# Second scores of each half between M2 and M7, in a fused cross-attention kernel on one core

## Chip, core and metric

One NeuronCore of one Trainium2 chip. The metric is the device time of one launch in microseconds. The kernel before took 1660.45 us, the median of three runs (1659.76 to 1660.83).

## What is computed

One perceiver layer on a state x of 256 rows by 512: a cross-attention of x over a context of 25088 rows (8 heads of 64), a self-attention of 16 heads, and a mixture of 8 experts. Only the cross-attention is touched. Cut to that:

```
q = heads(layernorm(x) @ Wq.T + bq)        # 256 rows, 8 heads of 64
k = heads(ctx @ Wk.T + bk)                 # 25088 rows
v = heads(ctx @ Wv.T + bv)
x = x + softmax(q @ k.T / sqrt(64)) @ v    # over all 25088 rows
x = x + self_attention(layernorm(x))       # not touched
x = x + experts(x)                         # not touched
```

## The kernel before

**Chunks.** The context is cut into 49 chunks of 512 rows. Step c (from -1 to 49, the middle ones in a hardware loop of two steps each) does the attention of chunk c and makes K and V of chunk c + 1. Every product of two fp32 matrices is taken as three fp16 products of a high and a low part; so each tile is split after it is made: ScalarE writes the high part (`block_highs`, `p_highs`, `ctx_highs`), VectorE the low part as the difference (`block_lows`, `p_lows`), and GpSimd the low parts of the context (`ctx_sums`, `ctx_lows`, lines 363 to 380).

**Strassen.** K (h = 0) and V (h = 1) of a chunk, four 256x256 blocks each, are made with Strassen's seven products, `units` M1, M5, M6, M2, M7, M3, M4 of 12 matmuls each, in four PSUM banks `ps_proj` (line 1147). Between them other engines work on the banks: ScalarE's `seed` (L527, L529; waits for M1) and `copy_m5` (L538; waits for M5), VectorE's `add_u4` (L877, L880; waits for M6 and copy_m5) and `add_c22` (L887; waits for M7). M7 waits for add_u4. M4 waits for c22_done, since it writes the bank that add_c22 reads. A block is done after M2 (C11), M7 and add_c22 (C22), M3 (C12), M4 (C21); then `block_highs` and `block_lows` (L549 to L554 and L861 to L867) take it out. The next half's M1, M5 and seed wait for the low parts of C11, C22 and C12.

**Attention of a chunk** goes in four groups g of two heads, two in each half (g = 2h and 2h + 1). TensorE's `scores` (L1193) fill the two banks `ps_s`, which are there once, so they wait for the exponentials of the group before. VectorE's `maxima` are a reduction (L839) and the running maximum nmax (L846). ScalarE's `exps` (L573) are four exponentials with sums, `p_highs` is L584, VectorE's `p_lows` L852. SP turns both parts of P with a transposing DMA (`turn_p`, L293) and TensorE's `weigh` (PV, L1211) uses them two groups later. VectorE's `add_o` adds the result.

**Order.** There is no planner; each engine runs its own list in the order of the code, and semaphores join them. Per half h, before (groups 2h and 2h + 1):

- TensorE: M1, scores(2h), M5, M6, PV, M2, M7, scores(2h+1), M3, PV, M4.
- VectorE: C21 low of the half before, maxima(2h), p_lows(2h-1), add_u4, add_o, p_lows(2h), add_c22, C11 low, maxima(2h+1), C22 low, C12 low.
- ScalarE: C21 high of the half before, seed, p_highs(2h-1), alpha, copy_m5, exps(2h), p_highs(2h), C11 high, ctx_highs of chunk c + 2, C22 high, C12 high, exps(2h+1).
- GpSimd in the K half: four context sums (L363, L364, L366, L368), three low parts (L380), the rescaling of the accumulator (L420 to L425), the difference of maxima (L435). In the V half: four low parts (L380), of which all but the first wait for ScalarE's ctx_highs, the rescaling and the difference.

Of the kernel before, what the change touches and what calls it, by code (L numbers as in the profile page):

```python
# [56 lines left out]
def exists(c, n, count=NCH):  # L57

    return not isinstance(c, int) or 0 <= c + n < count


def after(c, n, least=0):

    return not isinstance(c, int) or c + n >= least


def back(c, u, lag, per=NG):

    return (c, u - lag) if u >= lag else (c - 1, u - lag + per)


def layer(nc, x, ctxt, wq, wk, wv, bv, cols, w_in, wg, w1, w2, w3, out):
    with ExitStack() as ctx:
# [141 lines left out]
        M1, M5, M6, M2, M7, M3, M4 = (0, 0, 0), (3, 3, 3), (4, 4, 1), (1, 1, 0), (5, 5, 1), (6, 2, 2), (2, 6, 1)  # L215
# [5 lines left out]
        def units_through(g):  # L221

            return UNITS * g - 6
# [16 lines left out]
        C11, C22, C12, C21 = (0, 0, 0), (3, 1, 1), (2, 0, 1), (1, 1, 0)  # L240

        def half_bank(n):

            return ps_proj[:, n, :].rearrange("p (t k) -> p t k", t=2)
# [213 lines left out]
        def _(act):  # L458
# [7 lines left out]
            def ctx_highs(k, odd, half):  # L466

                if half == 0:
                    act.wait_ge(ctx_loaded[odd], 8 * k + (16 - 8 * odd))
                    act.activation(ctx_s[odd][0][:, 0:2, :, :].rearrange("p b t k -> p (b t) k"), ctx_f[odd][:, :, 0:QUARTER],  # L470
                                   ACT.Copy).then_inc(ctx_high, 1)
                else:
                    act.activation(ctx_s[odd][0][:, 2, :, :], ctx_f[odd][:, 2:4, QUARTER:CH], ACT.Copy).then_inc(ctx_high, 1)
                act.wait_ge(t_sum, 4 * k - 1 + half)
                act.activation(ctx_s[odd][0][:, 3 + 2 * half:5 + 2 * half, :, :], t_f[:, 2 * half:2 * half + 2, :, :],  # L475
                               ACT.Copy).then_inc(t_high, 1)
# [88 lines left out]
            def exps(c, g, odd):  # L565

                act.wait_ge(nmax_done, NG * c + g + 1)
                if g % 2 == 0 and after(c, -2):
                    act.wait_ge(scaled, 2 * (c - 2) + g // 2 + 1)
                for b in range(2):  # L570
                    for r in range(2):
                        col = 4 * g + 2 * b + r
                        ins = act.activation(prob[:, g % 2, (2 * b + r) * HC:(2 * b + r + 1) * HC],  # L573
                                             ps_s[:, b, r * HC:(r + 1) * HC], ACT.Exp, bias=nmax[odd][:, col:col + 1],
                                             scale=LOGIT_SCALE, accum_out=lsum[odd][:, col:col + 1])
                ins.then_inc(exp_done, 1)
# [9 lines left out]
            def step(c, odd):  # L586
                for h in range(2):
                    strassen = exists(c, 1) and after(c, 0)
                    if exists(c, h) and after(c, h - 1):
                        block_highs(c + h, 1 - h, C21, odd if h == 0 else 1 - odd)  # L590
                    if not after(c, 0):
                        for g in range(NG):
                            plain_highs(h, g)
                        weight_sum_highs(h)
                    if strassen:
                        seed(c + 1, h)
                    pc, pg = back(c, 2 * h, 1)
                    if exists(pc, 0):
                        p_highs(pc, pg)
                    if exists(c, -1) and h == 0:  # L600
                        alphas(c - 1, 1)
                    if exists(c, 0) and h == 1:
                        alphas(c, 0)
                    if strassen:
                        copy_m5(c + 1, h)
                    if exists(c, 0):
                        exps(c, 2 * h, odd)
                    if exists(c, 0):
                        p_highs(c, 2 * h)
                    if strassen:  # L610
                        block_highs(c + 1, h, C11, 1 - odd)
                    if exists(c, 2):
                        ctx_highs(c + 2, odd, h)
                    if strassen:
                        for which in (C22, C12):
                            block_highs(c + 1, h, which, 1 - odd)
                    if exists(c, 0):
                        exps(c, 2 * h + 1, odd)
                    if isinstance(c, int) and c == LOOP_END + 1:
                        act.wait_ge(tisa_arg, h + 1)  # L620
                        act.activation(tisa_e[:, h, :], tisa_e[:, h, :], ACT.Exp).then_inc(tisa_exp, 1)
# [81 lines left out]
        def _(dve):  # L703
# [145 lines left out]
            def p_lows(c, g):  # L849

                dve.wait_ge(p_high, NG * c + g + 1)
                dve.scalar_tensor_tensor(out=p_s[:, g % 2, 1, :], in0=prob[:, g % 2, :], scalar=P_SCALE, in1=p_s[:, g % 2, 0, :],  # L852
                                         op0=ALU.mult, op1=ALU.subtract).then_inc(p_low, 1)
# [29 lines left out]
            def add_c22(k, h):  # L883

                g = 2 * k + h
                dve.wait_ge(unit_done, units_through(g) + 5)
                dve.tensor_tensor(half_bank(bank(h, 3)), half_bank(bank(h, 1)), m5_f[:, :, :], ALU.add).then_inc(c22_done, 1)  # L887
# [20 lines left out]
            def step(c, odd):  # L908
                for h in range(2):
                    strassen = exists(c, 1) and after(c, 0)  # L910
                    if exists(c, h) and after(c, h - 1):
                        block_lows(c + h, 1 - h, C21, odd if h == 0 else 1 - odd)
                    if not after(c, 0):
                        for g in range(NG):
                            plain_lows(h, g)
                        if h == 0:
                            split_q()
                            bias_rows()
                        weight_sum_lows(h)
                    if exists(c, 0):  # L920
                        maxima(c, 2 * h, odd)
                    pc, pg = back(c, 2 * h, 1)
                    if exists(pc, 0):
                        p_lows(pc, pg)
                    if strassen:
                        add_u4(c + 1, h)
                    if exists(c, -1):
                        add_o(c - 1, h)
                    if exists(c, 0):
                        p_lows(c, 2 * h)  # L930
                    if strassen:
                        add_c22(c + 1, h)
                        block_lows(c + 1, h, C11, 1 - odd)
                    if exists(c, 0):
                        maxima(c, 2 * h + 1, odd)
                    if strassen:
                        for which in (C22, C12):
                            block_lows(c + 1, h, which, 1 - odd)
                    if isinstance(c, int) and c == LOOP_END + 1:
                        tisa_args(h)  # L940
                    if isinstance(c, int) and c == NCH and h == 0:
                        tisa_scores()
# [146 lines left out]
        def _(pe):  # L1089
# [126 lines left out]
            def step(c, odd):  # L1216
                for h in range(2):
                    if not after(c, 0):
                        for g in range(NG):
                            if h == 0 and g == 2:  # L1220
                                turn(0)
                            plain(h, g)
                        if h == 0:
                            project_q()
                    if isinstance(c, int) and c == NCH and h == 0:
                        tisa_scores()

                    def units(*which):
                        for m in which:
                            if exists(c, 1) and after(c, 0):  # L1230
                                unit(c + 1, 1 - odd, h, m)

                    for half, before, between, behind in ((0, (M1,), (M5, M6), (M2, M7)), (1, (), (M3,), (M4,))):
                        g = 2 * h + half
                        units(*before)
                        if exists(c, 0):
                            scores(c, g, odd)
                        units(*between)
                        vc, vg = back(c, g, PV_LAG)
                        if exists(vc, 0):  # L1240
                            weigh(vc, vg, odd if g >= PV_LAG else 1 - odd)
                        units(*behind)
# [139 lines left out]
```

## Time and profile before

| | |
|---|---|
| median of three runs | 1660.45 us |
| profiled execution | 1662.99 us, span 1661.3 us |
| TensorE matmuls busy | 1566.8 us (94%) |
| TensorE weight loads busy | 1276.5 us (77%) |
| VectorE busy | 1323.7 us (80%) |
| ScalarE busy | 1268.4 us (76%) |
| GpSimd busy | 822.6 us (50%) |
| mean granted TensorE clock | 0.971 of full speed |

The busy times are over the whole span; the steps of the Strassen loop lie between about 43 and 1277 us of it. Within that stretch each chunk repeats the one before almost to the hundredth of a microsecond, so a single chunk can be read on the timeline (here the stretch from 800 to 827 us, a V half and a K half).

### The profile page before, as it was taken

The numbers are of one execution on the slowest core, as the hardware profiler recorded it, in microseconds if no ns is written. First come the engines' busy times: TensorE is split into PE (matmuls) and PEld (weight loads), VectorE is DVE, ScalarE is ACT, GpSimd is POOL, SyncE is SP. The second block draws the span as 40 slices with busy tenths as digits, with TensorE's granted clock in tenths as the row PEclk, the third lists the DMA queues.
The fourth block names the chain that finished last, engine by engine and source line by source line (L and its number), as shares of the span: only waits on it lengthen the run. The fifth ranks groups of instructions, "written<-read, shape, count | busy, mean of one in ns | idle before, by whom it ended". The sixth has DMA issues, their size and how long they took to land.

```text
span 1661.3 us, 47795 instructions
## 1 busy us (share of the span) xinstructions
PE 1566.8 (94%) x17748; PEld 1276.5 (77%) x17748; DVE 1323.7 (80%) x1764; ACT 1268.4 (76%) x3074; POOL 822.6 (50%) x938
## 2 busy tenths in 40 slices
PE   7899999999999999999999999999998687999998
PEld 5788888888888888888888888888876455777776
DVE  7788888888888888888888888888887466766765
ACT  4888888888888888888888888888886254655554
POOL 5667657666676576666765766667653000000000
PEclk9999999999999999999999999999999765999999
DMA  4365454454544544545445445454456630555551
GB/s 171 80 136 129 107 139 112 122 133 108 137 126 107 139 110 123 134 111 134 126 107 139 111 123 133 108 137 126 109 106 157 167 151 1 191 204 210 192 198 43
DMA packets 442690, 216.03 MB, mean 130 GB/s; under 512 B 416768, under 2 KB 422912, under 8 KB 436112
## 3 DMA queue, kind: packets, MB, share of 16 engines
q1 hardware_dynamic: 442352, 215.07, 48.1%
q8 instruction: 34, 0.56, 0.2%
q10 hardware_dynamic: 288, 0.27, 0.1%
q14 instruction: 16, 0.13, 0.0%
HBM read 111.96 MB, written 0.56 MB: 68 GB/s over the span
## 4 chain that ended last, share of the span: by engine, by line
DVE 33%; PE 25%; ACT 20%; issue 18%; DMA 1%; SPq 1%; DVEq 1%; ACTq 0%; POOL 0%; POOLq 0%
ACT prob L573 14%; DVE cmax L839 12%; PE ps_proj L1316 9%; DVE p_s L852 6%; DVE nmax L846 5%; PE ps_o L1339 5%; PE ps_proj L1147 4%; ACT p_s L584 3%; DVE k_s L864 2%; DVE ps_proj L877 2%; DVE v_s L861 2%; PE ps_s L1193 2%; ACT v_s L549 1%; PE ps_proj L1176 1%; PE ps_s L1272 1%
## 5 line engine op out<-in xcount | busy, mean ns | idle before, releaser
L1147 PE MATMUL ps_proj<-ctx_s,wk_s 128*128 128x256 f16 x4032 | 487.9, 273 | 30.5 <-DVE ps_proj L877 27.6
L1147 PE MATMUL ps_proj<-wv_s,ctx_s 128*128 128x256 f16 x4032 | 483.5, 274 | 1.2 <-ACT ps_proj L529 1.2
L1147 PEld LDWEIGHTS ps_proj<-ctx_s,wk_s 128*128 128x128 f16 x4032 | 376.5, 98 | 103.7 <-issue 63.1
L1147 PEld LDWEIGHTS ps_proj<-wv_s,ctx_s 128*128 128x128 f16 x4032 | 381.3, 98 | 64.6 <-issue 20.0
L573 ACT ACTIVATE prob<-ps_s,nmax 128x256 f32<-128x256 f32 x784 | 360.4, 473 | 77.0 <-DVE nmax L846 72.5
L380 POOL TENSOR_TENSOR ctx_s<-t_f,ctx_s 128x512 f16<-128x512 f32 x192 | 220.0, 1157 | 358.9 <-ACT ctx_s L475 358.9
L852 DVE SCALAR_TENSOR_TENSOR p_s<-prob,p_s 128x1024 f16<-128x1024 f32 x196 | 291.1, 1485 | 57.6 <-ACT p_s L584 57.6
L839 DVE TENSOR_REDUCE cmax<-ps_s 128x4 f32<-128x1024 f32 x196 | 238.1, 1215 | 3.8 <-PE ps_s L1193 3.8
L584 ACT ACTIVATE p_s<-prob 128x1024 f16<-128x1024 f32 x196 | 209.1, 1067 | 6.7
L380 POOL TENSOR_TENSOR ctx_s<-ctx_f,ctx_s 128x512 f16<-128x512 f32 x144 | 167.1, 1160 | 69.2 <-ACT ctx_s L470 69.2
L1316 PE MATMUL ps_proj<-x_s,wsp 128*128 128x256 f16 x1536 | 180.5, 275 | 4.2 <-issue 3.2
L1316 PEld LDWEIGHTS ps_proj<-x_s,wsp 128*128 128x128 f16 x1536 | 151.2, 99 | 36.6 <-issue 3.5
L861 DVE TENSOR_TENSOR v_s<-ps_proj,v_s 128x512 f16<-128x512 f32 x192 | 127.1, 681 | 64.7 <-ACT v_s L549 64.7
L1211 PE MATMUL ps_o<-v_s,pt_s 128*128 128x64 f16 x4704 | 171.2, 194 | 6.6 <-DMA pt_s<-p_s 6.6
L1193 PE MATMUL ps_s<-k_s,q_s 64*128 64x256 f16 x2352 | 163.8, 272 | 13.9 <-ACT prob L573 8.9
L1211 PEld LDWEIGHTS ps_o<-v_s,pt_s 128*128 128x128 f16 x4704 | 165.0, 99 | 14.4 <-DMA pt_s<-p_s 7.8
L573 ACT ACTIVATION_READ_ACCUMULATOR prob<-ps_s,nmax 128x1 f32 x784 | 161.1, 205 | 0.0
L965 DVE SCALAR_TENSOR_TENSOR wsp<-wst,wsp 128x1024 f16<-128x1024 f32 x96 | 114.6, 1222 | 47.9 <-ACT wsp L645 47.9
L1193 PEld LDWEIGHTS ps_s<-k_s,q_s 64*128 64x128 f16 x2352 | 99.2, 94 | 68.1 <-ACT prob L573 35.6
L549 ACT ACTIVATE v_s<-ps_proj 128x512 f16<-128x512 f32 x192 | 114.1, 595 | 39.2 <-PE ps_proj L1147 37.8
L867 DVE TENSOR_TENSOR k_s<-ps_proj,k_s 128x512 f16<-128x512 f32 x144 | 94.4, 681 | 61.6 <-ACT k_s L554 61.6
L846 DVE SCALAR_TENSOR_TENSOR nmax<-cmax,nmax 128x4 f32<-128x4 f32 x196 | 116.0, 592 | 8.6
(163 smaller groups left out, 1875.5 us busy)
## 6 DMA issues: line engine op xcount, KB each, us to landing
ctx_f<-ctxt_dram SPq DMA_DIRECT2D x48, 1024.0 KB, 5.1
wst<-w_dram SPq DMA_DIRECT2D x96, 512.0 KB, 4.7
pt_s<-p_s SPq DMA_TRANSPOSE x392, 2.7
w_in_sb<-w_in_dram SPq DMA_DIRECT2D x1, 3072.0 KB, 11.1
tisa<-tisa_scores SPq DMA_DIRECT2D x3, 1024.0 KB, 12.0
w_f<-wk_dram SPq DMA_DIRECT2D x2, 512.0 KB, 5.7
ctx_f<-ctxt_dram SPq DMA_DIRECT2D x2, 512.0 KB, 7.0
w_f<-wv_dram SPq DMA_DIRECT2D x1, 1024.0 KB, 9.9
```

The lines of the kernel that those rows point to most:

```text
L380: pool.tensor_tensor(out=low[:, n, :, :], in0=sources[n], in1=high[:, n, :, :], op=ALU.subtract).then_inc(ctx_low, 1)
L549: ins = act.activation(out_v(0, odd, i, j), ps, ACT.Copy)
L573: ins = act.activation(prob[:, g % 2, (2 * b + r) * HC:(2 * b + r + 1) * HC], ps_s[:, b, r * HC:(r + 1) * HC], ACT.Exp, bias=nmax[odd][:, ...
L584: act.activation(p_s[:, g % 2, 0, :], prob[:, g % 2, :], ACT.Copy, scale=P_SCALE).then_inc(p_high, 1)
L839: dve.tensor_reduce(cmax[:, g % 2, :], ps_s[:, :, :].rearrange("p b (r k) -> p (b r) k", r=2), AX, ALU.max).then_inc(cmax_done, 1)
L846: dve.scalar_tensor_tensor(out=nmax[odd][:, 4 * g:4 * g + 4], in0=cmax[:, g % 2, :], scalar=-LOGIT_SCALE, in1=nmax[1 - odd][:, 4 * g:4 * g ...
L852: dve.scalar_tensor_tensor(out=p_s[:, g % 2, 1, :], in0=prob[:, g % 2, :], scalar=P_SCALE, in1=p_s[:, g % 2, 0, :], op0=ALU.mult, op1=ALU. ...
L861: ins = dve.tensor_tensor(out_v(1, odd, i, j), ps, out_v(0, odd, i, j), ALU.subtract)
L1147: ins = pe.matmul(ps_proj[:, bank(h, role), sub * QUARTER:(sub + 1) * QUARTER], lhsT, rhs, start=(fresh and sub == 0 and t == 0 and i == 0 ...
L1193: ins = pe.matmul(ps_s[:, head, r * HC:(r + 1) * HC], q_s[a][rows, g, r * P:(r + 1) * P], k_s[odd][b][rows, g, r * HC:(r + 1) * HC], start ...
L1211: ins = pe.matmul(ps_o[:, vg // 2, col:col + DK], pt_s[:, vg, a, 4 * head + tile, :], v_s[vodd][b][:, tile, u * DK:(u + 1) * DK], start=(i ...
L1316: ins = pe.matmul(ps_proj[:, u % 2, m * T:(m + 1) * T], wsp[a][:, (u // 2) % 2, m, col:col + P], x_s[b][:, t, :], start=(t == 0 and k == 0 ...
```

## The change

In each half TensorE takes scores(2h+1) between M2 and M7; before they stood between M7 and M3. VectorE takes maxima(2h+1) ahead of p_lows(2h), and C11 low ahead of add_c22. ScalarE takes exps(2h+1) ahead of C22 high and C12 high. Which semaphore each operation waits for, and its count, stay as they are. The orders after are:

- TensorE: M1, scores(2h), M5, M6, PV, M2, scores(2h+1), M7, M3, PV, M4.
- VectorE: C21 low, maxima(2h), p_lows(2h-1), add_u4, add_o, maxima(2h+1), p_lows(2h), C11 low, add_c22, C22 low, C12 low.
- ScalarE: C21 high, seed, p_highs(2h-1), alpha, copy_m5, exps(2h), p_highs(2h), C11 high, ctx_highs, exps(2h+1), C22 high, C12 high.

```diff
@@ scalar, step @@
                     if exists(c, 2):
                         ctx_highs(c + 2, odd, h)
+                    if exists(c, 0):
+                        exps(c, 2 * h + 1, odd)
                     if strassen:
                         for which in (C22, C12):
                             block_highs(c + 1, h, which, 1 - odd)
-                    if exists(c, 0):
-                        exps(c, 2 * h + 1, odd)
@@ vector, step @@
                     if exists(c, 0):
+                        maxima(c, 2 * h + 1, odd)
+                    if exists(c, 0):
                         p_lows(c, 2 * h)
                     if strassen:
+                        block_lows(c + 1, h, C11, 1 - odd)
                         add_c22(c + 1, h)
-                        block_lows(c + 1, h, C11, 1 - odd)
-                    if exists(c, 0):
-                        maxima(c, 2 * h + 1, odd)
-                    if strassen:
                         for which in (C22, C12):
                             block_lows(c + 1, h, which, 1 - odd)
@@ tensor, step @@
-                    for half, before, between, behind in ((0, (M1,), (M5, M6), (M2, M7)), (1, (), (M3,), (M4,))):
+                    for half, before, between, behind in ((0, (M1,), (M5, M6), (M2,)), (1, (), (M7, M3), (M4,))):
```

## Rows read from the trace of the kernel before

**Rows 1.** The page's first line.

```profile
span 1661.3 us, 47795 instructions
```

**Rows 2.** Timeline 800 to 830 us, weight loads: start us, us, engine, line, count, [idle].

```profile
800.28 1.22 PEld L1147 LDWEIGHTS ps_proj<-ctx_s,wk_s 128*128 128x128 f16 x12
...
812.75 1.22 PEld L1147 LDWEIGHTS ps_proj<-wv_s,ctx_s 128*128 128x128 f16 x12
...
815.49 0.55 PEld L1193 LDWEIGHTS ps_s<-k_s,q_s 64*128 64x128 f16 x12 [0.21 <-ACT prob L573]
...
819.56 1.22 PEld L1147 LDWEIGHTS ps_proj<-ctx_s,wk_s 128*128 128x128 f16 x12
...
821.64 1.22 PEld L1147 LDWEIGHTS ps_proj<-ctx_s,wk_s 128*128 128x128 f16 x12 [0.86 <-issue]
...
823.07 0.55 PEld L1193 LDWEIGHTS ps_s<-k_s,q_s 64*128 64x128 f16 x12 [0.21 <-issue]
...
825.82 1.22 PEld L1147 LDWEIGHTS ps_proj<-ctx_s,wk_s 128*128 128x128 f16 x12
```

**Rows 3.** The same timeline, VectorE.

```profile
805.51 0.16 DVE L846 SCALAR_TENSOR_TENSOR nmax<-cmax,nmax 128x4 f32<-128x4 f32 x1
...
810.84 0.68 DVE L861 TENSOR_TENSOR v_s<-ps_proj,v_s 128x512 f16<-128x512 f32 x1
...
817.81 0.62 DVE L846 SCALAR_TENSOR_TENSOR nmax<-cmax,nmax 128x4 f32<-128x4 f32 x1
818.35 2.37 DVE L852 SCALAR_TENSOR_TENSOR p_s<-prob,p_s 128x1024 f16<-128x1024 f32 x1
820.65 0.87 DVE L877 SCALAR_TENSOR_TENSOR ps_proj<-ps_proj,bk_d,m_f 128x256 f32<-128x256 f32 x2
...
822.03 1.21 DVE L852 SCALAR_TENSOR_TENSOR p_s<-prob,p_s 128x1024 f16<-128x1024 f32 x1
823.17 0.70 DVE L887 TENSOR_TENSOR ps_proj<-ps_proj,m_f 128x512 f32<-128x512 f32 x1
823.78 0.87 DVE L864 SCALAR_TENSOR_TENSOR k_s<-ps_proj,bk_s,k_s 128x256 f16<-128x256 f32 x2
```

**Rows 4.** Timeline 1264.5 to 1268 us: scores and the reduction that waited for them.

```profile
1265.11 0.55 PEld L1193 LDWEIGHTS ps_s<-k_s,q_s 64*128 64x128 f16 x12 [0.21 <-issue]
...
1265.98 1.23 DVE L839 TENSOR_REDUCE cmax<-ps_s 128x4 f32<-128x1024 f32 x1 [0.24 <-PE ps_s L1193]
...
1267.24 0.91 DVE L846 SCALAR_TENSOR_TENSOR nmax<-cmax,nmax 128x4 f32<-128x4 f32 x1
```

**Rows 5.** Timeline 800 to 830 us, GpSimd.

```profile
811.09 1.16 POOL L380 TENSOR_TENSOR ctx_s<-t_f,ctx_s 128x512 f16<-128x512 f32 x1 [7.34 <-ACT ctx_s L475]
...
817.15 1.26 POOL L364 TENSOR_TENSOR t_f<-ctx_f 128x512 f32<-128x512 f32 x1
818.38 1.27 POOL L366 TENSOR_TENSOR t_f<-ctx_f,t_f 128x512 f32<-128x512 f32 x1
819.72 2.13 POOL L368 TENSOR_TENSOR t_f<-ctx_f,t_f 128x512 f32<-128x512 f32 x1
823.33 1.16 POOL L380 TENSOR_TENSOR ctx_s<-ctx_f,ctx_s 128x512 f16<-128x512 f32 x1 [1.48 <-ACT ctx_s L470]
```

**Rows 6.** The same timeline, ScalarE: first and last instruction of exps(0).

```profile
818.56 0.47 ACT L573 ACTIVATE prob<-ps_s,nmax 128x256 f32<-128x256 f32 x1
...
820.28 0.21 ACT L573 ACTIVATION_READ_ACCUMULATOR prob<-ps_s,nmax 128x1 f32 x1
```

**Rows 7.** Timeline 40 to 76 us, TensorE matmuls around its stall at 58.5 us.

```profile
60.58 0.83 PE L1193 MATMUL ps_s<-k_s,q_s 64*128 64x256 f16 x12 [2.10 <-ACT prob L573]
61.34 4.46 PE L1147 MATMUL ps_proj<-wv_s,ctx_s 128*128 128x256 f16 x24
...
66.34 2.79 PE L1147 MATMUL ps_proj<-wv_s,ctx_s 128*128 128x256 f16 x24
```

**Rows 8.** Windows: stretch, its length, TensorE busy (instructions), granted clock, DMA share, GB/s.

```profile
62.00:64.00 2.00, 2.00 (x11) 0.50 0.12 29
```

## The prediction

> **What bounds the kernel now.** The reading order is: the page's span, the list of who waited for whom, the timeline of one chunk. The span is 1661.3 us and the profiled execution 1662.99 us, 2.5 us above the median of the three timed runs [rows 1]. The Strassen steps are 48 (c from 0 to 47), each with a K half and a V half. I measure a half from the start of its predecessor's M4 to the start of its own M4, on the weight loads. The V half lasts 812.75 - 800.28 = 12.47 us, the K half 825.82 - 812.75 = 13.07 us, a chunk 25.54 us [rows 2]. TensorE is nearly full in it: its one large wait is M7 of the K half, which waits for VectorE's add_u4 (the weight load sat idle 0.86 us). Everything else of the K half is TensorE's own stream, and the V half has only 0.26 us more than that stream (below).
>
> **The part that gains.** Scores(2h+1) between M2 and M7 need exp(2h). In the K half M2's loads end at 819.56 + 1.22 = 820.78 and exp(0) at 820.28 + 0.21 = 820.49 [rows 2, 6], so the scores start at once, after the 0.21 us of issue that every group of scores shows. They fill the hole in which M7 waits for add_u4. M7 then comes 0.55 + 0.21 us behind the scores' start, where add_u4 has just finished; the separate 0.76 us of scores behind M7 go, and the small remainder with them. Were nothing else to change, a half would be TensorE's own stream: M4 to scores(2h) 2.74, to M2 4.07, M2 1.22, issue 0.21 = 8.24 us to scores(2h+1); M7 1.22 and then, as from 823.07 to 825.82, 2.75 us to M4. That is 12.21 us in either half, a saving of 25.54 - 24.42 = 1.12 us per chunk, 54 us in 48 [rows 2].
>
> **The part that costs.** M4 waits for c22_done, that is for VectorE's add_c22, because M4 writes the bank which add_c22 reads. Before, add_c22 stands directly behind p_lows(2h) and ends at 823.87, 1.95 us ahead of M4 [rows 2, 3]. After, VectorE is in order and add_c22 stands behind four things: the wait for scores(2h+1), maxima (a reduction and nmax), p_lows(2h), C11. TensorE needs 1.22 + 2.75 = 3.97 us from the start of the scores to the point where M4 is due. VectorE needs, from the same start:
> - until the scores can be read 0.87 us (scores issued 1265.11, a reduction that waited for them starts 1265.98) [rows 4];
> - reduction 1.26 us to the start of nmax (1265.98 to 1267.24) [rows 4], of which I carry 1.25;
> - nmax 0.16 us if nothing holds it, less 0.08 us by which the next operation starts early [rows 3];
> - p_lows 1.22 us, less 0.07 us by which the next starts early (822.03 + 1.21 against 823.17) [rows 3];
> - C11: 0.60 us to the next start for V (0.68 us at 810.84, less the overlap), 0.79 us for K (two instructions, 0.87 us, less the overlap) [rows 3];
> - add_c22 0.70 us, and 0.12 us until TensorE goes on (for add_u4: 820.65 + 0.87 = 821.52, M7 at 821.64) [rows 2, 3].
> The sum is 4.77 us for V and 4.96 us for K, so M4 is late by at least 0.80 and 0.99 us. The halves are 13.01 and 13.20 us at best: 26.21 us, 0.67 us longer than before. The wait has moved from M7 (0.65 us) to M4, and it has grown. Behind M4 on TensorE lies the next half's M1 and with it the next first scores, so the lateness closes into a loop: M4, M1, scores(2h), M5, M6, PV, M2, scores(2h+1), maxima, p_lows, C11, add_c22, M4.
>
> **What VectorE shares with GpSimd.** nmax takes 0.16 us at 805.51, 0.62 us at 817.81 and 0.91 us at 1267.24; p_lows takes 1.21 us at 822.03 and 2.37 us at 818.35. The long nmax at 817.81 ends at 818.43, as GpSimd's L364 does (818.41), and the long p_lows begins as L366 runs (818.38 to 819.65) and has its 1.2 us after it. The other way round, L368 takes 2.13 us, beginning at 819.72 inside that p_lows and ending 1.13 us behind its end [rows 3 to 5]. So each of these two-input operations waits for one of the other engine that is under way. The Trainium skill ("SBUF — State Buffer", section "SBUF: two separate sides") says the same as a rule: for such operations the port pair is an exclusive lock and "the other fully blocks". By that rule the trace agrees; without such a lock the change would cost only the 0.67 us per chunk of the list above, some 1692 us in all. What matters is what GpSimd does at the two new places.
>
> V half. GpSimd's next L380 starts 811.09 - 800.28 = 10.81 us behind M4, at most 0.26 us less when the V half's small waits go [rows 2, 5]. nmax(3) starts at 8.24 + 0.87 + 1.25 = 10.36 and p_lows at 10.44, both earlier. They go free, and L380 waits until 11.66. The V half is 13.01 us.
>
> K half. The delayed L380 shifts GpSimd's sums: L364 follows 817.15 - 811.09 = 6.06 us later, at 17.72, or 4.71 in the K half, and ends at 5.97 with L366 behind it. nmax(0) is due at 2.74 + 0.87 + 1.25 = 4.86, so it ends with L364 at 5.98; p_lows(3) then takes its 2.37 us, as before, to 8.27. From p_lows' end to the start behind add_u4 and add_o it is 822.03 - 820.72 = 1.31 us, so maxima(1) starts at 9.58 and nmax(1) at 10.83, 0.47 us later than the scores would allow. ScalarE starts exps(0) at 6.11 (0.13 us behind nmax, as 818.56 behind 818.43), and L380 for the next blocks follows 823.33 - 818.56 = 4.77 us later, at 10.88 [rows 3, 5, 6]. So nmax(1) slips ahead of it by 0.05 us, but p_lows(0), due at 10.91, finds L380 running: it waits until about 12.10 and ends at 13.32. Then C11 (0.79, less 0.07), add_c22 0.70 and 0.12: M4 at 14.86. TensorE itself was ready at 12.40 (M7 waits for add_u4 until 9.19), so it stands still for 2.46 us.
>
> **What is moved and costs nothing.** On ScalarE exps(2h+1) goes ahead of C22 and C12. nmax is there at about 10.5 to 11.0, ctx_highs end at about 10.6 to 11.8, so exps end by 13.8, before add_c22 lets C22 go at 14.7; in V by 12.5 before 12.9. C22, C12 and C21 of the half then fall in the next half's first 2 us, where M5 is due only at 3.5; that is the cover, and it costs if exps slip by more than 1 us. p_lows(2h) is 2 to 3 us later in its half, and with it, on SP's queue, its transposing DMA and in the K half the context load behind that. The PV that reads the tile stands a whole half later, which is the cover; the sums that read the load stand a chunk later. If that cover were gone, PV would be late by the same 2 to 3 us.
>
> **The sum.** 13.01 + 14.86 = 27.87 us per chunk, 2.33 us more than 25.54, in 48 chunks 112 us. 1663.0 + 112 = 1775 us for the profiled execution, 1772 us for the median.
>
> **Rivals.** Prices are per chunk, times 48, on the median.
> - *Light chain*: nmax and p_lows miss GpSimd everywhere, because L380 comes a tenth later than p_lows(0). Then 26.21 us per chunk if nothing at all blocks (+0.67, +32 us, 1692 us), and 13.01 + 13.66 if only maxima(1)'s late start stays (+54 us, 1715 us). For it: the race in K is decided by 0.05 us. Against: of the three nmax shown two are held, and of the three p_lows one, the one that falls among the sums of the K half [rows 3, 4].
> - *Double block and clock*: L380 wins against nmax(1) as well. nmax ends at 12.0, p_lows waits for the second L380 and ends about 14.4, the K half is 15.9 us (+162 us, 1822 us). Or the K half's stall of 2.46 us lowers TensorE's clock: behind a stall of 2.10 us the granted clock was 0.50, and two units took 4.46 us in place of 2.79 [rows 7, 8]. Once per chunk, 1.67 x 48 = 80 us on top of the forecast, 1852 us; once in every second, 1812 us. For it: the stall is longer than that one. Against: it is shared out over a half that is otherwise full.
> - *Faster*: M4 is not late at all. That needs add_c22 done within 3.97 us of the scores' start; it decides if VectorE's chain falls below that, 0.8 us less than the shortest durations of the trace. Then 12.21 us per half, 54 us less, 1606 us. Against: every term is a row, and none has slack.
>
> **How the numbers follow.** Forecast (1745 to 1795 us) 0.42, double block or clock (1795 to 1860) 0.28, light chain (1690 to 1745) 0.25, faster 0.03, within 0.2% 0.02. The 0.2% is about what a measurement of this kernel can tell from no change. 1700 to 1850 us leaves out the lower end of the light chain, the upper end of the clock case, and the last two cases, some 0.15 to 0.2.
>
> **What would show it.** In the profile after, M7's wait for L877 in the V half is nil and in K small, and a new wait of L1147 for VectorE's L887 stands in both halves, about 0.8 us for V and 2.5 us for K; the ratio of the two tells of GpSimd. p_lows(0) of K lasts 2.3 us or more, p_lows(2) 1.2 us. VectorE sits idle before L839, waiting for the scores, in V (about 1 us). A granted clock below 1.00 within the loop would mean the clock case. The prediction is wrong if M4 shows no wait for L887, or if the halves are both near 13 us.

## The result, and the profile after

The changed kernel takes 1758.67 us (median of 6 runs, 1757.47 to 1762.88) against 1660.64 us for the kernel before in the same comparison: a ratio of 1.0591, 95% interval 1.0577 to 1.0606. It is slower by 98 us; the prediction was 1772 us, 1700 to 1850. The profiled execution's span grew from 1661.3 us [rows 1] to 1755.8 us, by 94.5 us.

The list of who waited for whom, over 700 us of the loop in the kernel after (engine, line, released by: total us, times, longest). Lines from the PE loop on have moved up by one: L1146 are the Strassen products, L1192 the scores.

```profile
DVE cmax L839 <- PE ps_s L1192: 81.2, 76, 2.4
PE ps_proj L1146 <- DVE ps_proj L887: 60.2, 51, 2.0
PEld ps_proj L1146 <- POOL ctx_s L380: 51.1, 25, 2.1
```

The wait of M4 for add_c22 (L887), which did not stand in the list before for these 700 us, is now TensorE's largest: 60.2 us in some 25 chunks, 2.4 us each. (The third line is the same stall of the K half seen from the weight loads and put down to GpSimd, whose operation merely ended last by the profile; the matmuls' line names L887.) VectorE now waits for the scores, which it never did in this stretch before.

The timeline of the kernel after, a V half and the K half behind it. Weight loads first, as in [rows 2]: M4 of K, M4 of V, scores(0), scores(1), M7 with M3, M4 of K.

```profile
808.16 1.22 PEld L1146 LDWEIGHTS ps_proj<-ctx_s,wk_s 128*128 128x128 f16 x12 [2.04 <-POOL ctx_s L380]
...
821.09 1.21 PEld L1146 LDWEIGHTS ps_proj<-wv_s,ctx_s 128*128 128x128 f16 x12 [0.56 <-DVE ps_proj L887]
...
823.82 0.55 PEld L1192 LDWEIGHTS ps_s<-k_s,q_s 64*128 64x128 f16 x12 [0.21 <-issue]
...
829.32 0.55 PEld L1192 LDWEIGHTS ps_s<-k_s,q_s 64*128 64x128 f16 x12 [0.21 <-ACT prob L573]
...
830.24 1.76 PEld L1146 LDWEIGHTS ps_proj<-ctx_s,wk_s 128*128 128x128 f16 x17 [0.37 <-issue]
...
835.68 1.22 PEld L1146 LDWEIGHTS ps_proj<-ctx_s,wk_s 128*128 128x128 f16 x12 [2.05 <-POOL ctx_s L380]
```

The V half lasts 821.09 - 808.16 = 12.93 us (12.47 before), the K half 835.68 - 821.09 = 14.59 us (13.07 before), the chunk 27.52 us against 25.54. From the first to the last M4 of a K half are 47 chunks; they took 1208.97 us before and take 1307.96 us now, 99.0 us more, and what follows them became 5.2 us shorter. 47 times 1.98 us is 93 us of it. Most of the rest is TensorE's clock: in six of the 47 V halves the granted clock fell to half of full speed behind the K half's stall, and each of the six lasted 14.55 us in place of 12.93, 10 us in all. The first and last chunks of the loop grew by about 4 us less than the others would. One of the six, M4 of K and M1 of V, and the window of granted clock (stretch, length, busy, clock, DMA share, GB/s):

```profile
779.08 1.47 PE L1146 MATMUL ps_proj<-ctx_s,wk_s 128*128 128x256 f16 x12 [1.96 <-DVE ps_proj L887]
780.38 2.73 PE L1146 MATMUL ps_proj<-wv_s,ctx_s 128*128 128x256 f16 x12
```

```profile
782.00:784.00 2.00, 2.00 (x18) 0.54 0.81 336
```

VectorE in the V half, to set against [rows 3]: the wait for the scores, nmax and p_lows free, add_c22 last.

```profile
817.27 1.23 DVE L839 TENSOR_REDUCE cmax<-ps_s 128x4 f32<-128x1024 f32 x1 [1.49 <-PE ps_s L1192]
...
818.53 0.16 DVE L846 SCALAR_TENSOR_TENSOR nmax<-cmax,nmax 128x4 f32<-128x4 f32 x1
818.61 1.22 DVE L852 SCALAR_TENSOR_TENSOR p_s<-prob,p_s 128x1024 f16<-128x1024 f32 x1
...
818.80 2.05 POOL L380 TENSOR_TENSOR ctx_s<-t_f,ctx_s 128x512 f16<-128x512 f32 x1 [7.42 <-ACT ctx_s L475]
...
820.35 0.69 DVE L887 TENSOR_TENSOR ps_proj<-ps_proj,m_f 128x512 f32<-128x512 f32 x1
```

And in the K half: nmax(0) held, p_lows(3) held, nmax(1) free, p_lows(0) held by an L380 that began 0.03 us before it; then C11 and add_c22, which ends 0.12 us before M4's loads.

```profile
826.04 0.99 DVE L846 SCALAR_TENSOR_TENSOR nmax<-cmax,nmax 128x4 f32<-128x4 f32 x1
...
826.96 2.37 DVE L852 SCALAR_TENSOR_TENSOR p_s<-prob,p_s 128x1024 f16<-128x1024 f32 x1
...
831.88 0.16 DVE L846 SCALAR_TENSOR_TENSOR nmax<-cmax,nmax 128x4 f32<-128x4 f32 x1
831.93 1.16 POOL L380 TENSOR_TENSOR ctx_s<-ctx_f,ctx_s 128x512 f16<-128x512 f32 x1 [1.47 <-ACT ctx_s L470]
831.96 2.21 DVE L852 SCALAR_TENSOR_TENSOR p_s<-prob,p_s 128x1024 f16<-128x1024 f32 x1
...
834.09 0.86 DVE L864 SCALAR_TENSOR_TENSOR k_s<-ps_proj,bk_s,k_s 128x256 f16<-128x256 f32 x2
834.88 0.68 DVE L887 TENSOR_TENSOR ps_proj<-ps_proj,m_f 128x512 f32<-128x512 f32 x1
```

### The profile page after: what moved, and what is told of

Same layout as the page of the kernel before. It is cut to its first block, busy times and chain, and to the rows that moved or that the text cites. A ratio compares the mean times of both kernels' runs of the same rounds, so it can differ in the third digit from the quotient of the medians.

```text
span 1755.8 us, 47795 instructions
## 1 busy us (share of the span) xinstructions
PE 1580.6 (90%) x17748; PEld 1288.3 (73%) x17748; DVE 1345.1 (77%) x1764; ACT 1279.2 (73%) x3074; POOL 912.0 (52%) x938
## 4 chain that ended last, share of the span: by engine, by line
PE 52%; DVE 27%; issue 15%; ACT 2%; DMA 2%; SPq 1%; DVEq 1%; POOL 0%; POOLq 0%; ACTq 0%
PE ps_proj L1146 26%; DVE cmax L839 10%; PE ps_proj L1315 9%; PE ps_s L1192 7%; PE ps_o L1338 4%; DVE ps_proj L887 3%; DVE p_s L852 3%; DVE k_s L864 2%; DVE ps_proj L877 2%; PE ps_o L1210 2%; DVE v_s L861 2%; DVE o_acc L895 2%; PE ps_proj L1175 1%; PE ps_s L1271 1%; DVE nmax L846 1%
## 5 line engine op out<-in xcount | busy, mean ns | idle before, releaser
L1146 PE MATMUL ps_proj<-ctx_s,wk_s 128*128 128x256 f16 x4032 | 480.8, 273 | 96.3 <-DVE ps_proj L887 88.3
L1146 PE MATMUL ps_proj<-wv_s,ctx_s 128*128 128x256 f16 x4032 | 489.7, 276 | 21.9 <-DVE ps_proj L887 20.6
L1146 PEld LDWEIGHTS ps_proj<-ctx_s,wk_s 128*128 128x128 f16 x4032 | 380.4, 98 | 165.2 <-POOL ctx_s L380 89.9
L380 POOL TENSOR_TENSOR ctx_s<-t_f,ctx_s 128x512 f16<-128x512 f32 x192 | 305.3, 1600 | 370.9 <-ACT ctx_s L475 370.9
L1146 PEld LDWEIGHTS ps_proj<-wv_s,ctx_s 128*128 128x128 f16 x4032 | 383.2, 99 | 93.2 <-DVE ps_proj L887 26.2
L852 DVE SCALAR_TENSOR_TENSOR p_s<-prob,p_s 128x1024 f16<-128x1024 f32 x196 | 334.9, 1709 | 2.0 <-ACT p_s L584 2.0
L380 POOL TENSOR_TENSOR ctx_s<-ctx_f,ctx_s 128x512 f16<-128x512 f32 x144 | 166.6, 1157 | 70.3 <-ACT ctx_s L470 70.3
L1192 PE MATMUL ps_s<-k_s,q_s 64*128 64x256 f16 x2352 | 166.0, 275 | 5.6 <-ACT prob L573 5.6
L1192 PEld LDWEIGHTS ps_s<-k_s,q_s 64*128 64x128 f16 x2352 | 100.1, 95 | 58.8 <-issue 32.6
L549 ACT ACTIVATE v_s<-ps_proj 128x512 f16<-128x512 f32 x192 | 108.5, 591 | 44.2 <-PE ps_proj L1146 24.9
L554 ACT ACTIVATE k_s<-ps_proj 128x512 f16<-128x512 f32 x144 | 80.8, 596 | 70.1 <-DVE ps_proj L887 44.7
```

The costliest lines, as they stand in the source:

```text
L380: pool.tensor_tensor(out=low[:, n, :, :], in0=sources[n], in1=high[:, n, :, :], op=ALU.subtract).then_inc(ctx_low, 1)
L549: ins = act.activation(out_v(0, odd, i, j), ps, ACT.Copy)
L1146: ins = pe.matmul(ps_proj[:, bank(h, role), sub * QUARTER:(sub + 1) * QUARTER], lhsT, rhs, start=(fresh and sub == 0 and t == 0 and i == 0 ...
L1192: ins = pe.matmul(ps_s[:, head, r * HC:(r + 1) * HC], q_s[a][rows, g, r * P:(r + 1) * P], k_s[odd][b][rows, g, r * HC:(r + 1) * HC], start ...
```

## The experiments

The theory: from the start of scores(2h+1) TensorE needs 3.97 us until M4 is due, and add_c22 comes later than that because VectorE runs maxima, p_lows and C11 ahead of it; in the K half p_lows is held by GpSimd on top. The main rival: the scores' new place on TensorE, or ScalarE's new order, is what costs. Each kernel was compared with the kernel before on the same chip (1661.73 us for the first, third, fifth and sixth below, 1660.22 us for the others). Differences to the changed kernel go across these comparisons, so 1 or 2 us in them mean nothing. Lengths of halves are those of most chunks of the loop. All compute the whole layer.

### TensorE's order alone

```diff
 # the kernel before, and only:
-  ((0, (M1,), (M5, M6), (M2, M7)), (1, (), (M3,), (M4,)))
+  ((0, (M1,), (M5, M6), (M2,)), (1, (), (M7, M3), (M4,)))
```

> Only TensorE's order is the changed one; VectorE and ScalarE keep the order before. Theory (the loss sits on VectorE between scores(2h+1) and M4): no wait of M4 for add_c22; but the reduction of maxima(2h+1) now stands behind add_c22, which waits for M7, so from scores(2h+1) to the reduction it is some 3.5 us in place of 1.45, exps(2h+1) end later, and scores(2h) of the next half wait for them: about 7.5 + 5.5 = 13.0 us for V and 13.3 us for K, 26.35 us per chunk, some 1700 us, slower than before by 40 and faster than the changed kernel by 60. Rival (the scores' new place by itself is what costs, as it pushes M7 back by 0.76 us): as slow as the changed kernel, 1759 us. Second rival (nothing but the saving counts): 54 us less than before, 1606 us.

Measured: 1716.26 us, ratio 1.0333 (1.0311 to 1.0355). It is slower than before, as expected, and faster than the whole change, so neither rival holds. Where the time goes, in its timeline: the second nmax of the K half is held by GpSimd, exps(1) begin late, and scores(2) of the V half wait for them.

```profile
809.66 1.03 DVE L846 SCALAR_TENSOR_TENSOR nmax<-cmax,nmax 128x4 f32<-128x4 f32 x1
...
810.72 0.47 ACT L573 ACTIVATE prob<-ps_s,nmax 128x256 f32<-128x256 f32 x1 [1.60 <-DVE nmax L846]
...
812.71 0.55 PEld L1193 LDWEIGHTS ps_s<-k_s,q_s 64*128 64x128 f16 x12 [1.38 <-ACT prob L573]
```

M4 has no wait for L887 in this kernel, and the wait is where it was expected. The time is 16 us above the expectation: the K half lasts 13.33 us, as expected, the V half 13.46 us in place of 13.0. The expectation left out that GpSimd holds nmax by almost 1 us in both halves (1.03 here, 1.07 in the next); as the K half fits all the same, its other terms were taken too long, and how much the hold costs was not tried. The move on TensorE without VectorE's maxima moved too costs 55 us.

### VectorE's and ScalarE's orders alone

```diff
 # the changed kernel, and only:
-  ((0, (M1,), (M5, M6), (M2,)), (1, (), (M7, M3), (M4,)))
+  ((0, (M1,), (M5, M6), (M2, M7)), (1, (), (M3,), (M4,)))
```

> VectorE's and ScalarE's orders of the change; TensorE's order is the one before, so scores(2h+1) come behind M7, 9.46 us behind M4 in place of 8.24. Theory (VectorE's chain of 4.8 to 5.0 us from these scores to M4 sets the half): V 14.2 and K 15.1 us where GpSimd holds nothing, 29.3 us per chunk and 1840 us; with nmax and p_lows held in both halves 15.4 and 16.8 us, 1980 us. Between them, about 1910 us. Rival (what costs in the change is the scores' new place on TensorE): faster than the changed kernel, below 1759 us.

Measured: 1906.62 us, ratio 1.1478 (1.1454 to 1.1501). The time is the one expected, the way to it is not. The theory's direction stands: with the scores 1.2 us later the same chain makes M4 later still, and the rival (faster than 1759 us) falls. But p_lows(2h) is not held in the chunk looked at, and the K half is 14.76 us long, not 15.1 or more. What was not in the expectation is TensorE's clock. The matmuls of that kernel: M1 of a V half, later the K half's M4 behind its stall; and the windows of granted clock (stretch, length, busy, clock, DMA share, GB/s).

```profile
799.76 2.77 PE L1146 MATMUL ps_proj<-wv_s,ctx_s 128*128 128x256 f16 x12
...
829.05 1.47 PE L1146 MATMUL ps_proj<-ctx_s,wk_s 128*128 128x256 f16 x12 [2.31 <-DVE ps_proj L887]
830.36 1.47 PE L1146 MATMUL ps_proj<-wv_s,ctx_s 128*128 128x256 f16 x12
```

```profile
800.00:802.00 2.00, 2.00 (x11) 0.50 0.64 262
...
830.00:832.00 2.00, 2.00 (x23) 1.00 0.70 188
```

The same M1 takes 2.77 us in one chunk, at half clock, and 1.47 us in the next, at full clock. The second is the exception: the V half lasts 15.9 us or more in 44 of 47 chunks, and 14.24 us only in this one. Over the loop the granted clock is 0.94 to 0.95 of full. At full clock a chunk is 14.24 + 14.76 = 29.0 us, near the 29.3 expected where GpSimd holds nothing; the other 1.67 us per chunk, some 73 us in all, are the clock. The middle value of about 1910 us stood for holds by GpSimd between none and all. In this chunk only the two nmax of the K half are held (1.19 and 0.45 us), and that half is still shorter than the 15.1 us expected without any. So it is luck that 1910 us was hit.

### add_c22 and C11 ahead of p_lows

```diff
 # the changed kernel, VectorE:
   maxima(c, 2 * h + 1, odd)
-  p_lows(c, 2 * h)
-  block_lows(c + 1, h, C11, 1 - odd)
   add_c22(c + 1, h)
+  block_lows(c + 1, h, C11, 1 - odd)
+  p_lows(c, 2 * h)
```

> The changed kernel with VectorE's order maxima(2h+1), add_c22, C11 low, p_lows(2h): p_lows and C11 no longer stand ahead of add_c22. Theory (M4 waits for VectorE's chain through p_lows and C11): add_c22 can start with M7's end, 2.3 us behind the scores' start, and ends at 3.0 against 3.97 us when M4 is due. No wait of M4 for L887 in either half, halves of 12.2 and 12.4 us, 24.6 us per chunk, about 1616 us, faster than both kernels. Rival (the exps moved ahead of C22 and C12 on ScalarE, or p_lows being late, hold the loop): within 20 us of the changed kernel's 1759.

Measured: 1624.81 us, ratio 0.9784 (0.9763 to 0.9806). Faster than both. In its timeline add_c22 of the K half follows nmax at once, M4 has no wait, and p_lows is still held by GpSimd (1.84 us), now where it delays nobody:

```profile
799.21 1.84 DVE L852 SCALAR_TENSOR_TENSOR p_s<-prob,p_s 128x1024 f16<-128x1024 f32 x1
...
811.90 1.22 PEld L1148 LDWEIGHTS ps_proj<-wv_s,ctx_s 128*128 128x128 f16 x12
...
822.42 0.70 DVE L887 TENSOR_TENSOR ps_proj<-ps_proj,m_f 128x512 f32<-128x512 f32 x1
...
823.81 1.84 DVE L852 SCALAR_TENSOR_TENSOR p_s<-prob,p_s 128x1024 f16<-128x1024 f32 x1
...
824.20 1.22 PEld L1148 LDWEIGHTS ps_proj<-ctx_s,wk_s 128*128 128x128 f16 x12
```

The K half is 824.20 - 811.90 = 12.30 us, and so is the V half: TensorE's own stream, which was worked out as 12.21 us; p_lows(0) comes again after 823.81 - 799.21 = 24.60 us, as expected. The chunk is 0.94 us shorter than before, 44 us in 47, of which 37 us arrive. The rest goes at the ends of the loop: its first four chunks are 1.9 us shorter in place of 3.8, and its last three are 3.1 us longer than before. Why was not followed further.

### p_lows last, C11 still ahead of add_c22

```diff
 # the changed kernel, VectorE:
   maxima(c, 2 * h + 1, odd)
-  p_lows(c, 2 * h)
   block_lows(c + 1, h, C11, 1 - odd)
   add_c22(c + 1, h)
+  p_lows(c, 2 * h)
```

> The changed kernel with p_lows(2h) moved behind add_c22 and nothing else (VectorE: maxima(2h+1), C11 low, add_c22, p_lows(2h)). Theory (p_lows, 1.2 to 2.2 us, is the term of the chain that makes M4 late; C11's 0.6 to 0.8 us alone fit into the 3.97 us): the chain from the scores' start is 3.6 us for V, and 12.5 us behind M4 for K where M4 is due at 12.4: halves of 12.3 and 12.5 us, 24.8 us per chunk, about 1630 us. Rival (C11 ahead of add_c22 costs its own length whatever stands elsewhere): 1.4 us per chunk more than with both behind, about 1690 us.

Measured: 1634.18 us, ratio 0.9826 (0.9798 to 0.9854). Moving p_lows alone takes back more than the whole loss: 1759 to 1634 us, 2.6 us per chunk. C11 ahead of add_c22 then costs some 7 us (the ratios 0.9826 and 0.9784), and not evenly. In 29 of 47 K halves M4 comes after 12.30 us as with add_c22 first: C11 fits into TensorE's time. In 16 it comes after 13.05 us, and in each of these GpSimd's L380 holds nmax(1), which starts level with it (to 0.02 us). In all but the last of the 29 the two start as level, and nmax(1) takes its 0.16 us: the same race goes both ways within one kernel. One of the 16:

```profile
829.38 1.17 DVE L846 SCALAR_TENSOR_TENSOR nmax<-cmax,nmax 128x4 f32<-128x4 f32 x1
829.38 1.16 POOL L380 TENSOR_TENSOR ctx_s<-ctx_f,ctx_s 128x512 f16<-128x512 f32 x1
...
832.09 1.47 PE L1148 MATMUL ps_proj<-ctx_s,wk_s 128*128 128x256 f16 x12 [0.59 <-DVE ps_proj L887]
```

### C11 behind add_c22, p_lows still ahead

```diff
 # the changed kernel, VectorE:
   maxima(c, 2 * h + 1, odd)
   p_lows(c, 2 * h)
-  block_lows(c + 1, h, C11, 1 - odd)
   add_c22(c + 1, h)
+  block_lows(c + 1, h, C11, 1 - odd)
```

> The changed kernel with add_c22 ahead of C11 low again, all else the same (VectorE: maxima(2h+1), p_lows(2h), add_c22, C11 low). Theory (each term ahead of add_c22 is paid in full): 0.60 us less in the V half and 0.79 us less in the K half, M4's wait 0.0 to 0.1 and 1.2 us, 1.4 us per chunk, about 67 us less, 1692 us. Rival (M4's wait is for M7's end or for ScalarE and not for the length of the chain): no change, 1759 us.

Measured: 1667.32 us, ratio 1.0035 (1.0025 to 1.0045). The direction is the theory's, the size is not: 91 us less than the changed kernel where 67 were expected. The V half fell from 12.93 to 12.33 us, the 0.60 us expected, the K half from 14.59 to 13.38 us, 1.21 where 0.79 were expected, and the clock no longer falls in the loop (10 us). The timeline of the K half shows what else moved.

```profile
826.32 1.15 POOL L380 TENSOR_TENSOR ctx_s<-ctx_f,ctx_s 128x512 f16<-128x512 f32 x1 [0.26 <-ACT ctx_s L470]
826.33 1.16 DVE L846 SCALAR_TENSOR_TENSOR nmax<-cmax,nmax 128x4 f32<-128x4 f32 x1
827.41 1.21 DVE L852 SCALAR_TENSOR_TENSOR p_s<-prob,p_s 128x1024 f16<-128x1024 f32 x1
827.43 2.21 POOL L380 TENSOR_TENSOR ctx_s<-t_f,ctx_s 128x512 f16<-128x512 f32 x1
```

With the V half shorter, nmax(0) met the end of a shorter overlap (0.37 us in place of 0.99) and maxima(1) started on time. nmax(1) now comes 0.01 us behind L380 and is held 1.16 us, but then p_lows, 0.02 us ahead of the second L380, runs free, and it is that L380 which takes 2.21 us. So only one operation in the chain is held, and the chain started half a microsecond earlier. M4 of K waits 0.93 us for L887, not 1.2.

### GpSimd kept away from p_lows

```diff
 # the changed kernel, ctx_lows:
+  if n == 0 and after(k, -2):
+      pool.wait_ge(p_low, NG * (k - 2) + 1)
```

> The changed kernel; GpSimd's first low part of the K half's three (L380) waits until p_lows(2h) of that half is done, so that the two cannot meet; nothing is left out. Theory (p_lows(0) is held by L380 for 1 us in each K half, and that is on the path to M4): p_lows(0) falls from 2.2 to 1.2 us, the K half from 14.6 to 13.6 us, the V half stays 12.9, about 47 us less, 1712 us. Rival (the long p_lows is not on the path, or is long for a reason of its own): no change, 1759 us, and p_lows(0) still 2.2 us.

Measured: 1707.12 us, ratio 1.0279 (1.0255 to 1.0303), 52 us less than the changed kernel, 47 expected. The K half fell from 14.59 to 13.60 us, 47 us in 47 chunks, and the granted clock is 1.00 over the loop, so that the six slow V halves are gone as well (10 us; the first and last chunks give some 4 us back). Its lines from L378 on stand two higher: p_lows is L854, L380 is L382.

```profile
826.40 1.22 DVE L854 SCALAR_TENSOR_TENSOR p_s<-prob,p_s 128x1024 f16<-128x1024 f32 x1
...
827.70 1.16 POOL L382 TENSOR_TENSOR ctx_s<-ctx_f,ctx_s 128x512 f16<-128x512 f32 x1 [2.79 <-DVE p_s L854]
...
829.13 0.89 PEld L1148 LDWEIGHTS ps_proj<-ctx_s,wk_s 128*128 128x128 f16 x9 [1.06 <-POOL ctx_s L382]
```

A wait added to GpSimd makes the kernel faster: its idle time before this operation grew from 1.47 to 2.79 us. The same p_lows takes 1.22 us and not 2.21, and M4's loads wait 1.06 us and not 2.05: the microsecond that GpSimd's operation held VectorE is paid one for one by TensorE.

### ScalarE's order

```diff
 # TensorE as changed, VectorE maxima, add_c22, C11, p_lows; ScalarE as before:
   ctx_highs(c + 2, odd, h)
-  exps(c, 2 * h + 1, odd)
   for which in (C22, C12):
       block_highs(c + 1, h, which, 1 - odd)
+  exps(c, 2 * h + 1, odd)
```

> TensorE's order of the change, VectorE's order maxima(2h+1), add_c22, C11 low, p_lows(2h), and ScalarE with the order before: exps(2h+1) behind C22 and C12 high. Theory (ScalarE's part of the change is worth nothing while exps(2h+1) end before the next scores(2h) are due): exps start 4.1 and end 6.1 us behind scores(2h+1), the next scores are due at 6.7: no change against the same kernel with exps first, 1625 us (1615 to 1635). Rival (the exps' move is needed for the gain): scores(2h) wait for exps as in the kernel where TensorE's order alone was changed, about 1 us per half, 1700 us or more.

Measured: 1624.97 us, ratio 0.9783 (0.9767 to 0.98), within the intervals the same as with the exps first (1624.81 us, 0.9784). ScalarE's part of the change is worth nothing in that kernel. In the changed kernel itself it was not tried alone.

## Why the prediction was right

**Where it is lost.** The loop named (M4, M1, scores(2h), ..., p_lows, C11, add_c22, M4) is the one the profile after shows, with the wait at M4 for L887. The floor of 0.80 us for V measured 0.44 us on the matmuls and 0.56 us on the loads; the V half came out at 12.93 for 13.01 us. The wait is smaller than the half tells because TensorE's own stream is 12.30 us and not 12.21: M7 and M3 in a row take 2.52 us (817.16 to 819.68), and they were added up as 2.43.

**The K half, step by step**, all from M4 of V (821.09):

| | predicted | measured |
|---|---|---|
| nmax(0) ends, held by L364 | 5.98 | 5.94 |
| p_lows(3) ends | 8.27 | 8.24 |
| scores(1) start | 8.24 | 8.23 |
| M7 starts, behind add_u4 | 9.19 | 9.15 |
| maxima(1) start | 9.58 | 9.54 |
| nmax(1) starts, free | 10.83 | 10.79 |
| L380 starts | 10.88 | 10.84 |
| p_lows(0) ends | 13.32 | 13.08 |
| M4 starts | 14.86 | 14.59 |

The race of 0.05 us came out as worked out. The hold of p_lows(0) was mis-sized, 2.21 us in all and not 2.4, in two parts. L380 was taken to start only when nmax(1) was done, and it started beside nmax's last 0.11 us, so that it was done at 12.0 and not at 12.1. And p_lows was taken to need its whole 1.22 us behind L380, where it ended 1.08 us behind it. The rows before say so too: the held p_lows ends at 820.72, 1.07 us behind L366 (819.65), which was read as "its 1.2 us" [rows 3, 5]. That is 0.24 of the 0.27 us of the K half, and with V's 0.08 us the chunk is 0.35 us shorter than forecast, 17 us: 1772 becomes 1755, measured 1759.

That the rest is only 4 us is in part luck. The forecast took 48 equal chunks at full clock. The clock fell in six V halves, which adds 10 us; the first and last chunks grew less than the others, and what follows the loop became 5.2 us shorter, which takes about as much away.

**The gain** on TensorE is real, 0.94 us per chunk in place of 1.12 (halves of 12.30 us with add_c22 first), and it was worth less than what add_c22's place cost.

**The rivals.** The light chain did not happen in the changed kernel; with GpSimd's operation held back it did, at 1707 us for the 1715 worked out. Its odds were argued with "of the three p_lows one"; [rows 3] show two, and of the four p_lows of the chunk one is held, of the four nmax three. The double block did not happen: where nmax(1) did lose the race (C11 behind add_c22), p_lows then won against the second L380 and ran free. Its pattern was taken from [rows 3, 5], where GpSimd's L366 wins behind L364; behind an L380 VectorE won, with recorded starts as close. Why the two differ is open. The clock case happened in six of 47 chunks, for 1.62 us each where 1.67 were worked out: the stall before M4 is 1.96 us, shorter than the 2.46 forecast, and the granted clock over the loop is 0.99. By the prediction's own words, a clock below 1.00 within the loop, that case showed, for 10 us in place of 80. With stalls of 2.31 us (VectorE's and ScalarE's orders alone) the clock falls in nearly every chunk.

**What was said to cost nothing.** ScalarE's reordering was, as far as tried. VectorE's idle time ahead of the reduction in V is 1.49 us for the 1 us foretold; it waits there while add_c22 is not yet possible, and pays for it afterwards. The transposing DMA behind the later p_lows made no PV wait between 400 and 1100 us.

## What to carry to other kernels

When an operation is moved forward on one engine, count, on each engine that follows, what now stands ahead of the operation that the first engine needs next; here one reordering of VectorE's list separated a loss of 98 us from a gain of 37 us. Operations whose result is needed soonest go first, the long one with half a period of slack (p_lows) goes last. Where two engines hold each other up, work out who starts first to some hundredths of a microsecond, and keep both outcomes in the range, for a change elsewhere may turn the race.

## What the runs showed of the hardware

A two-input VectorE operation on SBUF and one of GpSimd's run one after the other, whichever is under way first (where both had just finished an operation, GpSimd's L366 came first behind L364 and VectorE's p_lows behind L380: see the double block): an operation of four elements per partition takes 0.16 us alone and 1.16 us behind an L380; p_lows takes 1.22 and 2.21 us. The held operation is shown as busy for the whole time. C11's low part, one of whose inputs lies in PSUM, was not held: it took 0.86 us (834.09) while an L380 was under way. Starting GpSimd's operation 1.3 us later gave 52 us. TensorE's clock stayed at full behind stalls of 1.96 us in 41 of 47 chunks and fell to half in six (0.99 over the loop); with stalls of 1.75 us in the V half and 2.31 us in the K half it fell in nearly every chunk (0.94 to 0.95), and with stalls of 1.0 us (GpSimd kept away) it did not fall (1.00). Whether the longest stall or the idle time of a chunk in sum decides, no run here separates.
